# Two z projections in one piece, sums behind them, and other portions for an interleaved inverse

## What is computed

```python
mixed = hidden_states @ w_qkv
z = (hidden_states @ w_z).reshape(B, S, HV, DV)
y = conv_general_dilated(x, conv_w, ...)   # 4 taps along the sequence
mixed = silu(y); q, k, v = split(mixed)
q = _l2norm(q) * DK ** (-0.5); k = _l2norm(k)
def step(Sm, inp):                          # 128 steps
    Sm = Sm * exp(g_)
    kv = einsum('bhk,bhkv->bhv', k_, Sm)
    delta = (v_ - kv) * b_
    Sm = Sm + einsum('bhk,bhv->bhkv', k_, delta)
    o = einsum('bhk,bhkv->bhv', q_, Sm)
og = o * silu(z)
on = og * rsqrt(mean(og * og) + EPS) * norm_w
out = on.reshape(B, S, VAL_DIM) @ w_out
```

## Time and profile before

| | |
|---|---|
| median of 3 runs | 2225.94 us (2223.59 to 2243.5) |
| the profiled execution | 2234.28 us, span 2232.4 us |
| PE busy | 2020.2 us, 90% of the span |
| DVE busy | 1787.1 us, 80% |
| ACT busy | 1458.0 us, 65% |
| POOL busy | 872.1 us, 39% |

### The profile page before, as it was taken

The page is one execution under the profiler, slowest core; times in us unless marked ns, Lnnn a source line. Parts: engine busy times, 40 slices in busy tenths (PEclk is TensorE's granted clock), DMA queues, the critical chain, the costliest instruction groups (busy, mean ns, idle before and its releaser), DMA issues.

```text
span 2232.4 us, 48707 instructions
## 1 busy us (share of the span) xinstructions
PE 2020.2 (90%) x18444; PEld 1603.0 (72%) x18444; DVE 1787.1 (80%) x3136; ACT 1458.0 (65%) x2819; POOL 872.1 (39%) x586
## 2 busy tenths in 40 slices
PE   4648999999999999999999999998876899999998
PEld 3436787878888788887887888776764467666777
DVE  6789898998989989898898988976335777767765
ACT  4545766778777676776777777764766656565632
POOL 1623444354443544443444444421343123313232
PEclk8869999999999999999999999998999999999999
DMA  3422322333233323322233223121252021222232
GB/s 77 95 70 54 78 43 73 74 63 71 59 73 71 67 65 65 71 64 65 72 61 78 43 75 83 39 50 43 55 178 88 1 79 64 104 95 76 88 138 87
DMA packets 274629, 161.52 MB, mean 72 GB/s; under 512 B 209352, under 2 KB 246752, under 8 KB 269280
## 3 DMA queue, kind: packets, MB, share of 16 engines
q1 hardware_dynamic: 274400, 158.41, 27.5%
HBM read 122.43 MB, written 35.91 MB: 71 GB/s over the span
## 4 chain that ended last, share of the span: by engine, by line
PE 54%; DVE 26%; issue 7%; ACT 6%; DMA 3%; SPq 3%; POOL 2%; DVEq 0%; ACTq 0%; POOLq 0%
PE ps L1412 9%; PE ps L1414 7%; PE ps L1413 7%; DVE A L952 7%; PE ps L1798 4%; PE ps L1578 4%; PE ps L1543 4%; DVE BP L1164 3%; DVE TM L1012 3%; PE ps L1660 2%; PE ps L1682 2%; PE ps L1564 2%; ACT SC L899 2%; DVE UT L1000 2%; DVE TI L1016 2%
## 5 line engine op out<-in xcount | busy, mean ns | idle before, releaser
L952 DVE SCALAR_TENSOR_TENSOR A<-ps,CW,A 128x508 f32<-128x508 f32 (+2 forms) x768 | 515.1, 733 | 39.6 <-ACT A L705 37.2
L1412 PE MATMUL ps<-XH,WH 128*128 128x512 f32 x768 | 344.3, 448 | 70.4 <-DVE A L952 68.7
L523 POOL TENSOR_TENSOR EB<-EB,HJ 128x1024 f32<-128x1024 f32 x64 | 123.0, 1922 | 617.5 <-DMA EB<-decay_rows 617.5
L1413 PE MATMUL ps<-XL,WH 128*128 128x512 f32 x768 | 311.2, 405 | 0.0
L1414 PE MATMUL ps<-XH,WL 128*128 128x512 f32 x768 | 311.1, 405 | 0.0
L1543 PE MATMUL ps<-WO,SZ 128*128 128x256 f32 x1024 | 246.6, 386 | 17.5 <-ACT Q L718 9.3
L1412 PEld LDWEIGHTS ps<-XH,WH 128*128 128x128 f32 x768 | 150.7, 196 | 117.8 <-DVE A L952 61.8
L1543 PEld LDWEIGHTS ps<-WO,SZ 128*128 128x128 f32 x1024 | 195.0, 193 | 52.3 <-issue 16.3
L507 POOL TENSOR_TENSOR Y<-Y,DL 128x1024 f32<-128x1024 f32 x62 | 146.8, 2367 | 109.1 <-ACT DL L718 109.0
L899 ACT ACTIVATE SC<-ps,A 128x128 f32<-128x128 f32 x512 | 141.9, 384 | 59.1 <-DVE A L1317 58.4
L1414 PEld LDWEIGHTS ps<-XH,WL 128*128 128x128 f32 x768 | 150.1, 195 | 35.8
(11 more groups left out here) (217 smaller groups left out, 4740.7 us busy)
## 6 DMA issues: line engine op xcount, KB each, us to landing
EB<-decay_rows SPq DMA_DIRECT2D x128, 256.0 KB, 4.7
WE<-expert_halves SPq DMA_DIRECT2D x32, 1024.0 KB, 5.1
x_blocks<-BP SPq DMA_DIRECT2D x256, 32.0 KB, 1.6
X<-x_blocks SPq DMA_DIRECT2D x16, 512.0 KB, 5.0
tt_blocks<-TI SPq DMA_DIRECT2D x16, 512.0 KB, 2.6
tn_blocks<-TM SPq DMA_DIRECT2D x16, 512.0 KB, 2.6
TTF<-tt_blocks SPq DMA_DIRECT2D x256, 32.0 KB, 4.1
expert_halves<-BP SPq DMA_DIRECT2D x8, 1024.0 KB, 5.6
```

The costliest lines, as they stand in the source:

```text
L952: dve.scalar_tensor_tensor(acc, ps(i, 0, [[128, 4], [1, 128 - s]]), at(CW, tile * 4 + 3 - s, [[1, 1]]), acc, ALU.mult, ALU.add).then_inc(s ...
L1412: pe.matmul(out, sa, ma, start=(kt == 0), stop=False)
L1413: pe.matmul(out, sa, mb, start=False, stop=False)
```

## The change

Three places in the code:

- PE: `z_proj(m, 1)` moves from behind `og_sums` to behind `z_proj(m, 0)`. `og_sums_tr(k)` moves from ahead of the products with TA to behind `v_proj(vn, 0)`.
- ACT: `z_silu(m, 0)` and `z_silu(m, 1)` both stand ahead of the copy of the row of sums; before, one stood behind it and the other behind the two copies of U1.
- DVE: the room of the second portion of the inverse, for steps 8 to 63, becomes 3000 for n % 4 == 0 to 2 and 4000 for n % 4 == 3; it was 1500 for n % 4 == 0 and 4300 for the rest.

```diff
@@ ACT
+                    if s3:
+                        z_silu(m, 0)
+                        z_silu(m, 1)
                     if s4:
                         act.wait_ge(sem["og_mm"], k + 1)
...
-                    if s3:
-                        z_silu(m, 0)
                     if sv:
                         act.wait_ge(sem["u1"], vn + 1)
...
-                    if s3:
-                        z_silu(m, 1)
@@ DVE
-                    pump((1500 if n % 4 == 0 else 4300) if EARLY <= n < NSTEP else 0 if n == NSTEP else 5000 // rate)
+                    pump((4000 if n % 4 == 3 else 3000) if EARLY <= n < NSTEP else 0 if n == NSTEP else 5000 // rate)
@@ PE
                     if s3:
                         z_proj(m, 0)
+                        z_proj(m, 1)
...
                     if s4:
                         og_sums(k)
-                    if s3:
-                        z_proj(m, 1)
-                    if s4:
-                        og_sums_tr(k)
...
                     if sv:
                         v_proj(vn, 0)
+                    if s4:
+                        og_sums_tr(k)
```

## The result

The changed kernel takes **2309.11 us** (median of 3 runs, 2304.77 to 2310.24) against 2225.94 before (2223.59 to 2243.5). The ratio on record is 1.0355, with a 95% interval of 1.0326 to 1.0384 (the two medians alone give 1.037): slower, and inside the range from 2250 to 2330. The profiled execution's span went from 2232.4 to 2307.4 us, by 75.0.

What follows compares the result with a forecast made beforehand. PE bounds phases 2 and 3; in 0 and 1 kq_proj waits for DVE's late v taps. Phases 1, 2, 3, 0, then ramp and tail: -23 - 2 + 18 + 70 - 1 = +62 on 2234.28, 2296 us; range 2250 to 2330.

Steps and rivals of the forecast that it cites:

- The lock: VectorE and GpSimd share SBUF ports exclusively: a DVE tensor_tensor or copy starting during a POOL tensor_tensor does not finish before it.
- the first rival: The longer portion of the inverse costs only its length, nothing more is caught behind POOL: 2234 us, chance 10%.
- Phase 0: Steps with n % 4 == 0: longer portion caught behind POOL, v_tap at 16.8 us, step 30.6 instead of 25.14, +70 us.
- one of the two signs: In phase 0: forecast wrong if the 64-wide multiplies X by TI keep their mean of 219 ns.
- count for early rows: Phase 0, as in n = 44: L507 ends at 14.5 us, the five added instructions follow until 17.0; 16.7 after phase 3's stand.
- The rule on which the number stood: Phase 0: with 10 instructions that can be caught instead of 6, DVE always has some left when L507 starts.
- Phase 1: Steps with n % 4 == 1: a sum and a multiply fewer ahead of v_tap, 22.46 us instead of 24.21, -23 us.
- its condition: Phase 1's gain holds where PE is slowed after a stall; otherwise v_proj waits for kq's last tap, gaining only 0.2 us.
- Phase 3: Steps with n % 4 == 3: late transpose and larger portion, v_tap at 13.5 us, PE stands 1.7 us, +18 us.
- rival 4: Inverse ends behind L854's turn, shifting store and loads, and phase 3 falls to the lower clock: 2326 or over, 11%.
- Phase 2, ramp and tail: Steps with n % 4 == 2: -0.13 us each, -2 us; ramp's few inverse portions +2; tail's z projection filling waits -3.
- hardly a reserve: Phase 3: the inverse ends 0.4 us before ScalarE's L854 wants it, 13.9 us in; no delay of the TTF loads.

Runs made afterwards that it cites:

- e3: The changed kernel with POOL's three instructions of phases 0 and 3, and the v and z weight splits, cut to 8 columns: 2214.30 us, ratio 0.9910.
- e5: The changed kernel with the last portion of the inverse in phase 2 at 3900 instead of 2900: 2269.92 us, ratio 1.0181.
- e6: The changed kernel with the second portion of phases 0 and 1 back at 1500 and 4500, as placed before the change: 2304.98 us, ratio 1.0341.
- e2: The kernel before with only the new second portion of the inverse, PE's and ACT's orders old: 2291.13 us, ratio 1.0251.
- e1: The changed kernel with the second portion of before, so PE's and ACT's new orders alone: 2250.66 us, ratio 1.0068.
- e7: The changed kernel with four portions of the inverse rebalanced, none ahead of v_tap in phase 0: 2208.49 us, ratio 0.9902.

## Why the prediction was right, and where it was off

**Direction and size.** The lock was the reason to leave the first rival (2234 us) for the forecast, and e3 shows it directly: with POOL's instructions small the same DVE instructions take their own length. The Trainium skill, page "SBUF — State Buffer", section "Who interferes with whom", describes the pair of ports that VectorE and GpSimd share as an exclusive lock, where the one that comes second is fully blocked. The runs agree, for both sides. In phase 3 of before DVE's 1024-wide multiply starts first and takes 1.22 us, and L596 takes 2.43; after, L596 starts first and takes 1.89, and the multiply takes 2.90. POOL's L579 takes 2.29 us where DVE's L1034 is under way and 1.65 where it isn't.

**Phase 0: right.** Predicted were `v_tap` at 16.8, 5.6 us of stand and 2.5 at the lower clock. Measured were 16.45, 4.95 on average (12 waits of the 84.2 us, less phase 3's), and 30.14 - 22.40 - 4.95 = 2.8. The sum, 30.6, is 0.5 too long, 5 us in all. But one of the two signs by which the prediction wanted to be told wrong did come. The 64-wide multiplies (L995) were not the ones caught: they take 0.22 us each in n = 44 (the row's 1.00 us holds four, with the gaps between them), as before, and 0.26 on average over 12 steps only because one of the 48 was caught. POOL's row came so early that the old portion's nine instructions took the three catches, and the added five ran behind L507 at their own length. The prediction's own count for early rows (n = 44, "the five follow") had said this, and its 16.7 us is near the 16.45 that came; the sign was taken from the other pattern, that of n = 48, and contradicts it. So the sign was wrong and the sum right. The rule on which the number stood, that DVE has some of the portion left when L507 starts and the rest follows its end, held in both cases, as e5 and e6 show.

**Phase 1: right, by its condition.** 22.41 for 22.46, no wait of `kq_proj`, as PE is slowed in phase 0 ahead of it. Where it isn't slowed the gain goes, as said; the size was off. I gave 0.2 us of gain, and in e3 the phase is 24.57, which is 0.4 worse than before.

**Phase 3: the mis-sized term.** +18 was predicted, +32.9 came. The stand was put at 1.7 and is 2.06 to 2.08: `v_tap` at 13.70 instead of 13.5, since L579 took 2.29 us and not the 1.65 that the sum used, being itself behind DVE's multiply, and L596 and with it the catch came later. That is 12 x 0.4 = 5 us. The other 10 are the lower clock, which I had given to rival 4 alone: every other step loses 1.6 us (26.58 for 25.01), with 0.94 as its granted clock. e2 splits the stand: with the new portions and the old orders it is 0.54 us, so the orders bring 1.5 of the 2.06: `v_tap` starts at 12.41 in n = 51 of e2, 1.3 us sooner (the moved transpose, costed at 1.1), and PE is there 0.2 later. The multiply takes 2.91 us there too; L596 catches it with either order.

**Phase 2, ramp and tail.** Every kernel with the new orders and an unhindered phase 2 (after, e1, e3, e5, e6) has 22.39 for 22.59: 0.20 a step, for 0.13 predicted. The ramp gave +5, not +2, because n = 11 is a phase 3 step like the others; it should have been in that term.

**Rival 4** was half true. The clock did fall in phase 3, in half of its steps. The inverse ended 0.16 us behind ScalarE's turn (its idle time ahead of L853 in n = 51), but the copy starts 13.8 us in, as before (13.9), so this cost nothing: what the forecast called hardly a reserve was none.

**The base.** The sum was made on 2234.28 us and the kernel came at 2309; what was over, 13 us, is phase 3's 15 and the ramp's 3 less phase 0's 5. Errors of both signs stand behind the 13. That the 8 us between the profiled execution and the median were luck of phase 0 no trace shows, as there is one trace of before; the kernel before took 2231.73 and 2229.56 us in its two later medians, so the first one, 2225.94, was itself a little low. What e6 shows is how much phase 0 hangs on the rows: the old portion costs 27.57 when POOL's row comes early in all steps.

**Open.** Why every second phase 3 step keeps the full clock was not settled: up to the stand both kinds look the same in the records, and in e6, with the same stand of 2.08 us, 2 of the 12 steps lose it instead of 6. Which of PE's and ACT's orders does what wasn't separated.

## What to carry to other kernels

Price background work that is slotted between due work by what runs on the engine it shares ports with at that time, not by its own length: here a portion of 3.6 us (e3) became one of 7.9, and moving such work to where no deadline is near gained 1% (e7), while making the portions more even lost 2.5% (e2). A portion moved out of one stage has two deadlines in the next (here `v_proj`'s and `kq_proj`'s), and both must be checked. A stand in one stage can set another into its bad pattern, so undoing only the edit in the stage that lost most (e6) won back half of that stage's loss, and less than the stage that took the work back then lost.

## What the runs showed of the hardware

- The wait behind the other engine does not show as idle time. It lies in the duration of the waiting instruction, so DVE's busy time rose from 270.07 to 343.95 us in phase 0, of which the five added instructions are 13 x 1.5 = 19.5 by their own length. In e3 with the same instructions on DVE it is 260.11.
- The order of two starts 0.07 us apart decides 1.7 us: L1034 at 1242.45 behind L596 at 1242.38 takes 2.90 us. It takes 1.23 when L596 is small (e3), and 1.23 when it starts 0.3 us ahead of L596 (e5, phase 3); L596 then takes 2.68 us instead of 1.89.
- A long record on POOL is not the time for which DVE is held. POOL's L614, a power of 16 columns, runs for 2.91 us from 1072.98 in n = 44 of after, and the five DVE multiplies with both inputs in SBUF that run inside it keep 0.19 to 0.23 us each.
- A stand of 2.06 us was followed by the lower clock in one step and not in the next of its kind. Windows of n = 51 and n = 47: before the stand, in it, and the 4.4 us behind it. The clock is the column ahead of the DMA share; 1.00 is 2.4 GHz, 0.50 is 1.2:

```profile
1233.52:1251.03 17.51, 17.42 (x212) 14.11 (x210) 16.18 (x21) 12.68 (x22) 12.96 (x7) 1.00 0.14 52
1251.03:1253.09 2.06, 0.00 (x1) 0.03 (x1) 2.06 (x5) 0.00 (x0) 0.00 (x0) 1.00 0.27 102
1253.09:1257.50 4.41, 4.41 (x12) 3.35 (x13) 2.06 (x5) 2.61 (x4) 0.00 (x0) 0.62 0.49 83
...
1151.40:1153.45 2.05, 0.00 (x0) 0.02 (x1) 2.05 (x5) 0.00 (x0) 0.00 (x0) 1.00 0.26 99
1153.45:1157.90 4.45, 4.44 (x27) 3.87 (x28) 2.08 (x5) 3.91 (x8) 0.00 (x0) 1.00 0.52 83
```

In phase 0, with a stand of 4.92 us, the clock falls in every step of the pattern.
